# Turning x1 as f16 parts one step later, and moving the input and base products of the scan among its eight steps

## The reference, cut to what matters

```python
x1 = x + ffn(adaln(x))                      # block-scaled gate, up, down products
# GRU cell, token by token
gi = x1 @ W_ih + b_ih;  gh = h @ W_hh + b_hh
r, z = sigmoid(i_r + h_r), sigmoid(i_z + h_z)
n = tanh(i_n + r * h_n);  h = (1 - z) * n + z * h
# mixture of low-rank experts on the GRU's outputs hs
logits = silu(hs @ rw1.T + rb1) @ rw2.T + rb2 + gates      # best 2 of 16
out = x1 + hs @ W.T + bias + experts(hs, logits)
```

## Time and profile before

| | us |
|---|---|
| median of 3 runs | 1797.59 |
| lowest, highest | 1797.26, 1799.63 |
| the profiled execution | 1797.46 |
| its span | 1795.7 |
| PE busy | 1588.7 (88%) |
| DVE busy | 1448.9 (81%) |
| ACT busy | 684.1 (38%) |
| POOL busy | 502.6 (28%) |

### The profile page before, as it was taken

One profiled execution on the slowest core, in us unless ns is written; L12 is line 12 of the kernel. 1 busy time (PEld: TensorE's weight loads), 2 busy tenths in 40 slices (PEclk: granted clock), 3 DMA queues, 4 the chain that ended last, 5 costly groups with the idle time before them and its releaser, 6 DMA issues.

```text
span 1795.7 us, 76317 instructions
## 1 busy us (share of the span) xinstructions
PE 1588.7 (88%) x32908; PEld 1243.1 (69%) x32908; DVE 1448.9 (81%) x5603; ACT 684.1 (38%) x1736; POOL 502.6 (28%) x572
## 2 busy tenths in 40 slices
PE   5531458999999999999999999999999999999986
PEld 2211126778777777778778777777778777878874
DVE  6968888888888888888888888888888888887654
ACT  2323224444433443444443344443444434443331
POOL 4645323222222222222222222222222222221001
PEclk8755679999999999999999999999999999999996
DMA  8413300000101000001000000000010100000000
GB/s 301 156 66 112 138 18 20 26 33 32 33 32 32 32 32 32 22 19 33 32 32 33 32 33 32 32 28 31 33 33 32 32 32 32 27 27 26 21 15 19
DMA packets 35409, 80.10 MB, mean 45 GB/s; under 512 B 4864, under 2 KB 5248, under 8 KB 34688
## 3 DMA queue, kind: packets, MB, share of 16 engines
q1 hardware_dynamic: 28080, 63.09, 10.3%
q10 hardware_dynamic: 6992, 12.13, 1.9%
HBM read 58.43 MB, written 16.78 MB: 42 GB/s over the span
## 4 chain that ended last, share of the span: by engine, by line
PE 75%; DVE 18%; issue 3%; ACT 2%; POOL 1%; DMA 1%; ACTq 1%; DVEq 0%; SPq 0%; POOLq 0%
PE ps_rn_turn L1274 23%; PE ps_gi L1168 11%; PE ps_z L1274 10%; PE ps_gate_up L1107 6%; PE ps_down L1125 6%; PE ps_base L1177 4%; PE ps_gate_up L1101 4%; PE ps_base L1221 3%; PE ps_route L1177 3%; DVE fe L784 1%; DVE gi L583 1%; DVE gi L585 1%; DVE ps_rn_turn L581 1%; PE ps_rn_turn L1116 1%; DVE ps_gi L566 1%
## 5 line engine op out<-in xcount | busy, mean ns | idle before, releaser
L1274 PE MATMUL ps_rn_turn<-hT,whh 128*128 128x32 f16 x16320 | 449.2, 176 | 37.2 <-DVE hT L722 37.1
L1274 PEld LDWEIGHTS ps_rn_turn<-hT,whh 128*128 128x128 f16 x16320 | 435.2, 96 | 63.8 <-DVE hT L722 56.8
L996 POOL TENSOR_TENSOR qf<-f8c,fe 128x512 bf16<-128x512 bf16 x128 | 135.6, 1059 | 887.2 <-DVE f8c L801 867.3
L1168 PE MATMUL ps_gi<-x1T,wih 128*128 128x128 f16 x4608 | 288.6, 219 | 1.2 <-ACT gi L537 1.2
L1168 PEld LDWEIGHTS ps_gi<-x1T,wih 128*128 128x128 f16 x4608 | 270.2, 98 | 25.6 <-issue 1.7
L546 ACT ACTIVATE r_tanh<-r_pre,scale_half 128x64 f32<-128x64 f32 x256 | 89.0, 348 | 459.2 <-DVE r_pre L742 459.2
L1274 PE MATMUL ps_z<-hT,whh 128*128 128x32 f16 x8160 | 243.2, 176 | 0.0
L1274 PEld LDWEIGHTS ps_z<-hT,whh 128*128 128x128 f16 x8160 | 222.7, 96 | 0.0
L537 ACT ACTIVATE gi<-ps_gi,b_i,scale_x 128x128 f32<-128x128 f32 x384 | 144.4, 456 | 193.2 <-PE ps_gi L1168 193.2
L736 DVE TENSOR_TENSOR r_half<-ps_rn_turn,gi 128x64 f32<-128x64 f32 x256 | 56.5, 221 | 137.9 <-PE ps_rn_turn L1274 137.7
L548 ACT ACTIVATE z_tanh<-z_pre,scale_half 128x64 f32<-128x64 f32 x256 | 89.0, 348 | 159.4 <-DVE z_pre L752 159.4
(11 more groups left out here) (196 smaller groups left out, 2604.5 us busy)
## 6 DMA issues: line engine op xcount, KB each, us to landing
wih<-in_x_steps ACTq DMA_DIRECT2D x32, 256.0 KB, 5.4
xin<-in_x_steps SPq DMA_DIRECT2D x32, 256.0 KB, 3.8
xres<-in_x_steps SPq DMA_DIRECT2D x32, 256.0 KB, 3.2
x_dram<-x SPq DMA_DIRECT2D x32, 256.0 KB, 2.2
x_in<-x_dram SPq DMA_DIRECT2D x32, 256.0 KB, 2.8
out_rows<-y SPq DMA_DIRECT2D x32, 256.0 KB, 2.0
wst<-in_ffn_w SPq DMA_DIRECT2D x12, 512.0 KB, 3.3
sg_gs<-in_ffn_w SPq DMA_DIRECT2D x12, 512.0 KB, 3.8
```

The costliest lines, as they stand in the source:

```text
L996: g.tensor_tensor(blocked(qf[:, :]), blocked(f8c[:, :]), spread(fe16[:, :]), ALU.mult).then_inc(qf_done, 1)
L1168: last = mm(ps_gi[:, j * P:(j + 1) * P], wih_parts[:, k, at:at + P], x1T[:, x, k, :], start=k + w + x == 0, stop=k == KD - 1 and w == 1)
L1274: last = mm(ps[:, (at + j) * 2 * B:(at + j + 1) * 2 * B], whh[:, k, u, gate * D + j * P:gate * D + (j + 1) * P], hx(t)[:, 2 * k:2 * k + 2, ...
```

## The change

The f16 split of x1 is made before the turn, on the tokens' side, from x1 itself (`x1_parts`, two parts in SBUF): ACT the high part, DVE the low part, still in step 7. PE turns the parts, eight f16 turns, in step 1 of the next tile, and one ACT copy of 1024 elements brings both to `x1T`. The input products move from steps 0 to 5 to steps 2 to 7 (12, 36, 24, 24, 24, 24), their evictions to steps 3, 5, 7, and the base products from steps 4 and 6 to steps 1 and 2, six each. `scale_x` is doubled, since tile i's scale is still read while the next one is written.

```diff
-        scale_x = sb("scale_x", [P, 2])
-        S_X, X_TO_WH = (scale_x[:, i:i + 1] for i in range(2))
+        scale_x = [sb(f"scale_x{u}", [P, 2]) for u in range(2)]
+        S_X, X_TO_WH = ([scale_x[u][:, i:i + 1] for u in range(2)] for i in range(2))
...
-        x1T = sb("x1T", [P, 2, KD, P], F16)
+        x1_parts, x1T = sb("x1_parts", [P, 2, D], F16), sb("x1T", [P, 2, KD, P], F16)
+        turn_x = ps_turn.bitcast(F16)
...
# ScalarE, step 7, tile e
-                    wait(act, x_ev, count(e, 1))
-                    wait(act, gi_ev, count(e, 3))
-                    nc.scalar.activation(scale_x[:, :], ps_x_scale, ACT.Copy).then_inc(x_scale_ok, 1)
-                    act.wait_ge(x_mm, count(e, 1, 1))
-                    wait(act, gi_mm, count(e, 3))
+                    wait(act, x_lo, count(e, 1))
+                    wait(act, gi_ev, count(e - 1, 3))
+                    nc.scalar.activation(scale_x[e % 2][:, :], ps_x_scale, ACT.Copy).then_inc(x_scale_ok, 1)
+                    act.wait_ge(x1_done, count(e, 1, 1))
+                    wait(act, x_mm, count(e, 1))
                     act.wait_ge(x_scale_ok, count(e, 1, 1))
-                    nc.scalar.activation(x1T[:, 0, :, :], ps_turn[:, :].rearrange("p (k n) -> p k n", k=KD),
-                                         ACT.Copy, scale=S_X).then_inc(x_hi, 1)
+                    nc.scalar.activation(x1_parts[:, 0, :], x1[:, :], ACT.Copy, scale=S_X[e % 2]).then_inc(x_hi, 1)
...
-                if I and s in (1, 3, 5):
-                    g = s // 2
+                if I and s == 1:
+                    act.wait_ge(x_mm, count(i, 1, 1))
+                    wait(act, gi_mm, count(i, 3))
+                    nc.scalar.activation(x1T[:, :, :, :], turn_x.rearrange("p (u k n) -> p u k n", u=2, k=KD),
+                                         ACT.Copy).then_inc(x_ev, 1)
+                if I and s in (3, 5, 7):
+                    g = s // 2 - 1
...
# VectorE
-                    wait(dve, x_mm, count(e, 1))
+                    wait(dve, x_lo, count(e, 1))
...
-                    v.scalar_tensor_tensor(x1T[:, 1, :, :], ps_turn[:, :].rearrange("p (k n) -> p k n", k=KD), S_X,
-                                           x1T[:, 0, :, :], ALU.mult, ALU.subtract).then_inc(x_ev, 1)
+                    v.scalar_tensor_tensor(x1_parts[:, 1, :], x1[:, :], S_X[e % 2], x1_parts[:, 0, :], ALU.mult,
+                                           ALU.subtract).then_inc(x_lo, 1)
...
# TensorE
             def turn_inter(f, n):
-                if n == 2:
+                if n == 3:
                     wait(pe, x_ev, count(f, 1))
...
-            def turn_x1(e):
-                pe.wait_ge(t_ev, count(e + 1, NF, 2))
-                for k in range(KD):
-                    last = turn_(ps_turn[:, k * P:(k + 1) * P], x1[:, k * P:(k + 1) * P], idf[:, :])
+            def turn_x1(i):
+                pe.wait_ge(x_lo, count(i, 1, 1))
+                pe.wait_ge(t_ev, count(i + 1, NF, 3))
+                for u in range(2):
+                    for k in range(KD):
+                        at = (u * KD + k) * P
+                        last = turn_(turn_x[:, at:at + P], x1_parts[:, u, k * P:(k + 1) * P], idh[:, :])
...
-            base_parts = {4: (0,), 6: (1, 2, 3)}
+            base_parts = {1: (0, 1), 2: (2, 3)}
...
-                if E and s == 7:
-                    turn_x1(e)
+                if I and s == 1:
+                    turn_x1(i)
...
-                if I and s < len(x_parts):
-                    x_wih(i, *x_parts[s])
+                if I and s >= 2:
+                    x_wih(i, *x_parts[s - 2])
```

More of the change, by code:

```diff
@@ L137, in build @@
         S_I, S_L, L_INV, S_WH_BY_I = (scale_l[:, i:i + 1] for i in range(4))
-        scale_x = sb("scale_x", [P, 2])
-        S_X, X_TO_WH = (scale_x[:, i:i + 1] for i in range(2))
-        idf, idb = sb("idf", [P, P]), sb("idb", [P, P], BF16)
+        scale_x = [sb(f"scale_x{u}", [P, 2]) for u in range(2)]
+        S_X, X_TO_WH = ([scale_x[u][:, i:i + 1] for u in range(2)] for i in range(2))
+        idf, idb, idh = sb("idf", [P, P]), sb("idb", [P, P], BF16), sb("idh", [P, P], F16)
         iota_b = sb("iota_b", [P, EXPERTS])
@@ L228, in build @@
                              "wl_low_part"))
-        x_small, x_row_ok, x_row_mm, x_scale_mm, x_scale_ok, x_hi = (
+        x_small, x_row_ok, x_row_mm, x_scale_mm, x_scale_ok, x_hi, x_lo = (
             sem(x) for x in ("x1_scale_steps", "x1_row_ready", "x1_maxima_in_row", "x1_scale_spread", "x1_scale_ready",
-                             "x1T_high_part"))
+                             "x1_high_part", "x1_low_part"))
         summed = sem("tile_in_block_sums")
@@ L537, in others @@
                         last = nc.scalar.activation(gi_gate(i, g)[:, k, :], ps_gi[:, k * P:(k + 1) * P], ACT.Identity,
-                                                    bias=b_i[:, g * KD + k:g * KD + k + 1], scale=X_TO_WH)
+                                                    bias=b_i[:, g * KD + k:g * KD + k + 1], scale=X_TO_WH[i % 2])
                     last.then_inc(gi_ev, 1)
@@ L939, in _ @@
             dve.wait_ge(first_consts, 32)
+            v.tensor_copy(idh[:, :], idf[:, :])
             v.tensor_copy(idb[:, :], idf[:, :]).then_inc(c_dve, 1)
```

## The result

The changed kernel takes 1818.12 us (median of 4 runs, 1817.55 to 1819.13) where the kernel before, on the same chip, takes 1797.42 (1796.44 to 1799.63): a ratio of 1.0113, 95% interval 1.01 to 1.0125. It is slower by 20.7 us. The profiled execution took 1817.9 us, its span is 1816.1.

The account below looks back on a forecast made before the run. Each scan step ends at the later of PE's side work and DVE's chain to hT. The terms sum to +0.75 us a tile, 20.3 us for 27 tiles, 21.3 with the ends: 1818.8 us, range 1808 to 1830.

Parts of the forecast that it names:

- step 7: Last step of a tile: 24 input products come (1.42), f32 turns go (0.55), PE sets the end; +0.87 us.
- step 0, with the gi wait: First step: 12 input products go, -0.70 us; DVE's new wait for the third gate's eviction adds +0.02.
- step 3: 12 input products come where PE sets the step's end; +0.71 us a tile.
- step 6: Nine base products go, 24 input products come; only 0.26 us stands before hT, so -0.20 us.
- steps 4 and 5: Three base products leave step 4; what it gains, step 5 waits: 0, at most -0.1 us.
- steps 1 and 2: Step 2's chain over POOL counts from step 1's hT, so it takes what step 1 gives; +0.05 us.
- The signs that the forecast named: Listed step windows; PE waiting for hT ending steps 0, 2, 4, 6; fe above 1 us; `r_half` released by PE.
- the first rival: fe finds POOL idle, so steps 1 and 2 really shorten, step 2 to 5.53 us; 1804 us, chance 0.06.
- The gi wait: DVE's step 0 start waits for the third gate's eviction, covered by PE's products; +0.02 us, bounds 0 and +0.5.
- The rest of the span: Outside the steady 27 tiles: tiles 0, 28, 29, 30 +3 us together, tiles 31 and after -2.
- The 81 ns for 128 columns: Rival: input products in steps 3 and 7 cost 81 ns each, 0.8 us a tile more; 1840 us, chance 0.02.

Follow-up runs that it names:

- b_turn8: The kernel before with the four f32 turns of x1 in step 7 made twice; 1811.82 us, ratio 1.0075.
- a_last12: The changed kernel with the third gate's input products dealt 36 and 12 over steps 6 and 7, not 24 and 24; 1804.68 us.
- a_turn16: The changed kernel with the eight f16 turns of step 1 made twice; 1820.58 us, ratio 1.0123.
- a_beta: The changed kernel with POOL's addition of beta moved from step 2 behind its qf product in step 3; 1814.3 us, ratio 1.0092.
- a_giwait: The changed kernel with DVE's step 0 wait split: two gates before r_half, the third only before n_pre; 1818.86 us, ratio 1.0114.
- a_deal: The changed kernel with its input products dealt 24, 24, 36, 12, 36, 12 over steps 2 to 7; 1788.31 us, ratio 0.9941.
- b_base12: The kernel before with only its base products moved, six each to steps 1 and 2; 1859.82 us, ratio 1.0342.
- b_base16: The kernel before with only its base products redealt, six in step 1 and six in step 6; 1808.64 us, ratio 1.0059.

## Why the prediction was right

It said 1818.8 us, range 1808 to 1830; measured 1818.12. Term by term, from the windows of one tile:

| term | forecast | measured |
|---|---|---|
| step 7 | +0.87 | +0.92 |
| step 0, with the gi wait | -0.68 | -0.66 |
| step 3 | +0.71 | +0.67 |
| step 6 | -0.20 | -0.16 |
| steps 4 and 5 | 0 | -0.02 |
| steps 1 and 2 | +0.05 | -0.03 |
| tile | +0.75 | +0.72 |

- The signs that the forecast named came, with two exceptions. The windows are within 0.1 us of those listed, fe in step 2 takes 1.15 us, and PE waits for hT in steps 2, 4 and 6. It does not wait in step 0: hT is there 0.10 us before PE is free, as the twelve products gave only their own price (0.66). And `r_half` stands 0.18 us behind the eviction's end, not within 0.1.
- Step 7: both prices were a little off and nearly cancelled. The turns that left were worth 0.44 us (`b_turn8`), not 0.55. The product costs less than the forecast's 0.059: step 3's twelve cost 0.67, 0.056 each, and twelve taken from step 7 gave 0.67 (`a_last12`). 24 x 0.056 - 0.44 = 0.90. That the term came out within 0.05 is in part luck.
- Steps 1 and 2: the coupling was right, and both arms of it were tried. More work in step 1 is taken back in step 2 (`a_turn16`), and with beta elsewhere step 2 falls to PE's end, 5.56 us (`a_beta`), close to the 5.53 that the first rival named. That rival did not come about in the changed kernel: fe came 0.16 us after beta had started (1020.10 against 1019.94), and this in nearly every tile. So thin a margin looks like luck, but the outcome did not hang on it alone: in tile 22 of `a_giwait` fe came first, and `finv` was held instead. As the forecast argued, all three small scales must pass; they do when beta is away or long over.
- The gi wait cost nothing, as said: the eviction ends at 1.70 us into the step, ahead of PE's products, and splitting the wait changed neither `r_half` nor the time (`a_giwait`). The 0.09 us by which `r_half` is late has another cause, still open, and PE's end of step 0 hides it.
- Tiles: the usual tile takes 47.17 us before and 47.92 after, the 0.75 of the forecast. That tiles 1 to 27 came to 18.9 us and not 20.3 is because some tiles are longer than the usual one, by 2.5 us in all in the profiled execution before (1.9 of it in one tile, below) and by 1.2 in the one after. The rest of the span grew by 1.5, forecast 1. These small misses partly cancel, so the 0.7 us between forecast and measured time is better than the terms deserve.
- The 81 ns for 128 columns of the Trainium skill (TensorE: Matmul & The Clock Gate, Back-to-back issue gap) would have made it 1840. The runs do not agree: 0.67 us for twelve products, 56 ns each.
- Incomplete in the forecast is the reason in step 4: I gave nothing for its three base products since step 5 would take it back. It took back 0.04 of 0.06 us. Most of the 0.65 us of work that left stands as a new wait of PE for hT at the end of step 4 itself, 0.60 at its weight loads, and `a_deal` shows that this wait can be used.

What stays open: whether fe is held because two engines need one port, as the Trainium skill has it (SBUF — State Buffer, Who interferes with whom), or by some other rule of order. The runs show that fe ends with POOL's instruction when it comes behind its start, that it is free without it, and that what follows fe is held when fe comes first; they show no more. Open too is why `r_half` is 0.09 us late in step 0.

## What to carry to other kernels

Where two engines alternate in setting the end of short steps, list for each step which comes last and by how much; work is free up to the other's end and costs its full price beyond it, so the same products dealt otherwise were worth 30 us here. Look for the step whose length follows from an event in the step before: time won ahead of it is lost in it, and the remedy is to move what holds it (one POOL instruction, some 22 us) rather than to deal the bound engine's work anew. Before counting on a wait of PE, try how much of it can be filled: the rows of products and of weight loads differ, and here neither was right in every step.

## What the runs showed of the hardware

PE's clock can fall behind short waits. In `b_base12` a wait of 1.6 us for hT came once a tile, and in every second tile half the clock was granted for part of the next step (mean 0.79 over it), at a cost of 1.3 us (8.11 for 6.81 in `b_base16`), 16.6 us in all. In the tiles between, the same wait (1.96 us in one) was followed by full clock. Half the clock was granted once, too, in the steady tiles of the kernel before, in tile 5, whose step 2 was longer than usual. Its steps 2 and 3:

```profile
535.60:541.60 6.00, 5.07 (x133) 4.43 (x131) 4.05 (x19) 3.67 (x10) 2.54 (x2) 1.00 0.02 4
541.60:549.10 7.50, 7.50 (x133) 5.24 (x134) 6.01 (x21) 1.04 (x3) 1.05 (x1) 0.77 0.01 2
```

PE was idle for 0.93 us in the one and ran at a mean granted clock of 0.77, between its two levels of 1.2 and 2.4 GHz, in the other: 7.5 us for the usual 5.90. The waits of 0.2 to 0.7 us that other tiles have did not bring it about. Nor does such a wait always: in tile 5 of `b_turn8` the same step has the same wait, and the next one runs at full clock and in its usual time:

```profile
538.90:544.94 6.04, 5.10 (x132) 4.45 (x130) 4.10 (x20) 3.67 (x10) 2.55 (x2) 1.00 0.02 4
544.94:550.85 5.91, 5.91 (x131) 4.75 (x132) 4.71 (x18) 1.04 (x3) 1.05 (x1) 1.00 0.01 3
```

So the length of one wait does not decide it, and what does stays open. A wait on the bound engine can cost more than its length, and moving PE's work out of a step can have a price that the distances between chains do not show.
